# Spreading the filter taps over an iteration, and sums of squares on ScalarE

## What is computed

```python
q, k, v = silu(causal_dwconv(x @ W, w))            # 4 taps each
q = q * rsqrt(sum(q*q, -1) + 1e-6)                 # per head; k likewise
delta_out = delta_rule_chunkwise(q, k, v, beta)    # triangular solves, then a scan
fir_s = causal_dwconv(v, fir_short_w)              # 3 taps
fir_l = causal_dwconv(v, fir_long_w)               # 31 taps
hid = gelu(concat([x, fir_s, fir_l, delta_out]) @ W_fuse1 + b_fuse1)
logits = hid @ W_fuse2 + b_fuse2                   # softmax -> weights of four paths
o = p0*fir_s + p1*fir_l + p2*delta_out + p3*v
o = o * rsqrt(mean(o*o, -1) + 1e-5) * norm_w       # per head
out = o @ W_o
```

## Time and profile before

| | us |
|---|---|
| median of three runs | 2076.14 (2073.52 to 2077.61) |
| the profiled execution | 2078.35 |
| its span, first to last instruction | 2076.5 |

### The profile page before, as it was taken

How to read it: one execution, slowest core, us unless ns; L and a number is a source line. 1 busy time by engine, 2 the same in 40 slices (tenths; PEclk the granted TensorE clock), 3 DMA queues, 4 the chain that set the end, 5 groups by cost and what they waited for, 6 DMA issues and landing times. The chain is left out here.

```text
span 2076.5 us, 22850 instructions
## 1 busy us (share of the span) xinstructions
PE 1713.4 (83%) x8588; PEld 1154.6 (56%) x8588; DVE 997.7 (48%) x2206; ACT 542.2 (26%) x1180; POOL 758.3 (37%) x948
## 2 busy tenths in 40 slices
PE   4248888897878888888627999999995899999997
PEld 2226565655556565656423666666664455555554
DVE  3625878778687878777471111111101344444332
ACT  3123341514243342512122111111111222221221
POOL 1754556484655546472202333333322111111100
PEclk9667889797988888796867999999998999999999
DMA  3010111020111010020032333223312000000000
GB/s 100 16 21 16 21 37 31 2 59 8 46 21 47 21 46 11 6 51 32 0 132 81 81 82 80 60 43 75 78 18 43 1 21 21 21 21 21 1 11 21
DMA packets 108318, 77.99 MB, mean 38 GB/s; under 512 B 57384, under 2 KB 101424, under 8 KB 108208
## 3 DMA queue, kind: packets, MB, share of 16 engines
q1 hardware_dynamic: 95920, 59.74, 10.0%
q0 software_dynamic: 12288, 16.79, 4.7%
HBM read 51.34 MB, written 25.17 MB: 37 GB/s over the span
## 5 line engine op out<-in xcount | busy, mean ns | idle before, releaser
L383 DVE SCALAR_TENSOR_TENSOR a_firT<-a_v_ch,a_fir_lw,a_firT 128x511 f32<-128x511 f32 (+14 forms) x480 | 359.0, 817 | 0.0
L1505 DVE TENSOR_SCALAR ex_y<-ps,gT 128x256 f32<-128x256 f32 x64 | 31.0, 484 | 409.1 <-PE ps L1460 409.1
L1460 PE MATMUL ps<-ex_w,ex_hT 128*128 128x256 f32 x1024 | 223.5, 379 | 0.0
L1449 PE MATMUL ps<-ex_xT,ex_w 128*128 128x512 f32 x512 | 222.1, 594 | 0.0
L1460 PEld LDWEIGHTS ps<-ex_w,ex_hT 128*128 128x128 f32 x1024 | 194.0, 190 | 29.5 <-issue 3.8
L1415 POOL DMA_INDIRECT acc_dram<-ex_y,idxT x64 | 100.0, 1562 | 294.0 <-DVE ex_y L1505 294.0
L1487 ACT ACTIVATE ex_hT<-ps 128x512 f32<-128x512 f32 x128 | 76.4, 597 | 368.3 <-PE ps L1449 368.3
L1449 PEld LDWEIGHTS ps<-ex_xT,ex_w 128*128 128x128 f32 x512 | 97.7, 191 | 119.6 <-issue 119.2
L675 POOL TENSOR_TENSOR a_prod<-a_Yp,a_spare 128x126 f32<-128x126 f32 (+22 forms) x248 | 145.6, 587 | 29.7 <-DMA a_Yp<-y_dram 10.6
L1067 PE MATMUL ps<-a_firT,a_w_f 128*128 128x512 f32 x256 | 128.9, 628 | 18.3 <-DVE a_firT L383 18.3
L677 POOL TENSOR_TENSOR a_spare<-a_spare,a_prod 128x126 f32<-128x126 f32 (+22 forms) x248 | 116.3, 469 | 19.4
(11 more groups left out here) (275 smaller groups left out, 3061.7 us busy)
## 6 DMA issues: line engine op xcount, KB each, us to landing
ex_w<-in_L_ffn_w SPq DMA_DIRECT2D x16, 1024.0 KB, 8.9
a_xa<-in_L_attn_hidden_states SPq DMA_DIRECT2D x8, 512.0 KB, 4.3
a_xr<-in_L_attn_hidden_states SPq DMA_DIRECT2D x8, 512.0 KB, 4.7
a_Yp<-y_dram SPq DMA_DIRECT2D x16, 256.0 KB, 3.8
acc_dram<-a_xr SPq DMA_DIRECT2D x8, 512.0 KB, 4.5
xn_dram<-a_gxn SPq DMA_DIRECT2D x8, 512.0 KB, 3.2
l_xw<-acc_dram SPq DMA_DIRECT2D x8, 512.0 KB, 3.9
out<-l_xw SPq DMA_DIRECT2D x8, 512.0 KB, 2.9
```

The lines of the kernel that those rows point to most:

```text
L383: nc.vector.scalar_tensor_tensor(out[:, kind, c, s:], v, w[:, c, n - 1 - s:n - s], out[:, kind, c, s:], ALU.mult, ALU.add).then_inc(fir_st ...
L1449: ins = nc.tensor.matmul(ps[:, n % 4, :], w1[j][:, c, f * P:(f + 1) * P], xT[j][:, c, half * 512:(half + 1) * 512], start=c == 0, stop=c = ...
L1460: ins = nc.tensor.matmul(dn_slot(n), hT[half][:, f, (n % 4) * CAP:(n % 4 + 1) * CAP], w2[j][:, f, :], start=f == 0, stop=f == FB - 1)
```

## The change

`FIR_EARLY` goes from 40 to 20. Four of the 20 early taps stand ahead of scan(3), 16 behind it, and nothing is left behind the routing scores. The other 48 are spread over the next repetition: 3, 3, 5, 2, 10, 6 and 7 at seven places of `join` (`rest_of`), 2 ahead of scan(1), 5 ahead of scan(2) and 5 ahead of the end of the filters, where 18 stood in `join` and 10 in `main`. On VectorE the first two mixes come ahead of conv(b, 2), the last two and o_sums(e, 0) behind conv(b, 0) and ahead of their sums, and the second `masked_loc` comes behind `route_stats`. ScalarE squares each head's 64 columns with an instruction of its own that also sums them (`accum_out`): eight a tile in `kq_out`, four a tile in `out_squares`, 48 a repetition where eight stood. VectorE's eight reductions a repetition go. The semaphores that counted them are renumbered, and the squares wait for the powers of the image before.

```diff
--- before.py
+++ after.py
@@ -101,7 +101,7 @@
 PROJ = (2, 3, 0, 1, 4, 5)
 PROJ_BANK = (4, 5, 2, 3, 0, 1)
 NFIR = 2 * (TAPS_S + TAPS_L)
-FIR_EARLY = 40
+FIR_EARLY = 20
 NSOLVE = 3 + 2 * 31
 
 
@@ -437,11 +437,7 @@
 
             def kq_sums(b, p):
 
-                for t in (2 * p, 2 * p + 1):
-                    dve.wait_ge(sq_ready, b * 4 + t + 1)
-                    nc.vector.reduce_sum(ss[:, 8 * t:8 * t + 8], sq[t % 2][:].rearrange("p (h c) -> p h c", c=DK),
-                                         axis=AX.X).then_inc(ss_ready, 1)
-                dve.wait_ge(ss_ready, b * 6 + 3 * p + 2)
+                dve.wait_ge(sq_ready, b * 4 + 2 * p + 2)
                 nc.vector.tensor_scalar(ss[:, 16 * p:16 * p + 16], ss[:, 16 * p:16 * p + 16], 1e-6, None, ALU.add).then_inc(ss_ready, 1)
 
             def betas(b):
@@ -472,10 +468,7 @@
                                             spread(causal, 1, 2), ALU.mult).then_inc(loc_ready, 1)
 
             def o_sums(e, p):
-                for t in (2 * p, 2 * p + 1):
-                    dve.wait_ge(osq_ready, e * 4 + t + 1)
-                    nc.vector.reduce_sum(so[:, H * t:H * t + H], by_head(osq[:, t, :]), axis=AX.X).then_inc(so_ready, 1)
-                dve.wait_ge(so_ready, e * 6 + 3 * p + 2)
+                dve.wait_ge(osq_ready, e * 4 + 2 * p + 2)
                 nc.vector.tensor_scalar(so[:, 8 * p:8 * p + 8], so[:, 8 * p:8 * p + 8], 1.0 / DK, 1e-5, ALU.mult, ALU.add).then_inc(so_ready, 1)
 
             def o_norm(e, p):
@@ -538,68 +531,76 @@
                                         spread(rs[d % 2][:, t, H:2 * H], 2, DK), ALU.mult).then_inc(d_ready, 1)
 
             def join(b, d, e, r):
+                k = [FIR_EARLY]
+
+                def rest_of(n):
+                    if d is not None:
+                        fir(d, k[0], k[0] + n)
+                        k[0] += n
+
                 if e is not None:
                     rest = softmax_in(e)
                 if r is not None:
                     route_prob(r)
                 if e is not None:
                     rest()
-                if b is not None:
-                    conv(b, 2)
-                if e is not None:
                     mix(e, 0)
                     mix(e, 1)
+                if b is not None:
+                    conv(b, 2)
+                if e is not None:
                     mix_sum(e, 0)
                     mix_sum(e, 1)
                 if b is not None:
                     conv(b, 3)
+                rest_of(3)
+                if b is not None:
+                    conv(b, 0)
+                    betas(b)
                 if e is not None:
                     mix(e, 2)
                     mix(e, 3)
-                if b is not None:
-                    conv(b, 0)
-                    betas(b)
+                    o_sums(e, 0)
+                rest_of(3)
                 if e is not None:
                     mix_sum(e, 2)
                     mix_sum(e, 3)
-                    o_sums(e, 0)
-                if d is not None:
-                    fir(d, FIR_EARLY, FIR_EARLY + 6)
                 if b is not None:
                     conv(b, 5)
                 if e is not None:
                     o_norm(e, 0)
                     o_sums(e, 1)
+                rest_of(5)
                 if b is not None:
                     kq_sums(b, 0)
+                if e is not None:
+                    o_norm(e, 1)
+                rest_of(2)
+                if b is not None:
                     kq_sums(b, 1)
-                if e is not None:
-                    o_norm(e, 1)
-                if d is not None:
-                    fir(d, FIR_EARLY + 6, FIR_EARLY + 14)
+                rest_of(10)
                 if b is not None:
                     scales(b)
                     masked_loc(b, 0)
                 if e is not None:
                     add_out(e, 0)
-                if b is not None:
-                    masked_loc(b, 1)
+                rest_of(6)
                 if e is not None:
                     add_out(e, 1)
                     route_stats(e)
+                if b is not None:
+                    masked_loc(b, 1)
                 if b is not None and b + 1 < B:
                     norm_stats(b + 1)
-                if d is not None:
-                    fir(d, FIR_EARLY + 14, FIR_EARLY + 18)
+                rest_of(7)
 
             def main(b, d, e, nxt):
                 k = [0]
 
                 def more(n):
                     if b is not None:
-                        hi = min(FIR_EARLY, k[0] + n)
-                        fir(b, k[0], hi)
-                        k[0] = hi
+                        fir(b, k[0], k[0] + n)
+                        k[0] += n
 
                 if d is not None:
                     scan(d, 0)
@@ -608,15 +609,17 @@
                 if e is not None:
                     route_rows(e)
                 if d is not None:
+                    fir(d, FIR_EARLY + 36, FIR_EARLY + 38)
                     scan(d, 1)
-                    fir(d, FIR_EARLY + 18, FIR_EARLY + 23)
+                    fir(d, FIR_EARLY + 38, FIR_EARLY + 43)
                     scan(d, 2)
-                    fir(d, FIR_EARLY + 23, NFIR)
+                    fir(d, FIR_EARLY + 43, NFIR)
+                more(4)
+                if d is not None:
                     scan(d, 3)
-                more(18)
+                more(FIR_EARLY - 4)
                 if e is not None:
                     route_scores(e)
-                more(FIR_EARLY)
 
             norm_stats(0)
             norm_rows(0)
@@ -649,11 +652,11 @@
                 pool.tensor_tensor(rstd[:], var[:, 0, :], mhalf[:, 0:NT], ALU.pow).then_inc(rstd_ready, 1)
 
             def o_pow(e, p):
-                pool.wait_ge(so_ready, e * 6 + 3 * p + 3)
+                pool.wait_ge(so_ready, e * 2 + p + 1)
                 pool.tensor_tensor(ro[:, 8 * p:8 * p + 8], so[:, 8 * p:8 * p + 8], mhalf[:, 0:8], ALU.pow).then_inc(ro_ready, 1)
 
             def kq_pow(b, p):
-                pool.wait_ge(ss_ready, b * 6 + 3 * p + 3)
+                pool.wait_ge(ss_ready, b * 2 + p + 1)
                 pool.tensor_tensor(rs[b % 2][:, 2 * p:2 * p + 2, :], ss[:, 16 * p:16 * p + 16].rearrange("p (t h) -> p t h", t=2),
                                    mhalf[:, 0:16].rearrange("p (t h) -> p t h", t=2), ALU.pow).then_inc(rs_ready, 1)
 
@@ -741,9 +744,12 @@
             def kq_out(b, t):
 
                 act.wait_ge(kq_ps, b * 4 + t + 1)
-                if t >= 2:
-                    act.wait_ge(ss_ready, b * 6 + t - 1)
-                nc.scalar.activation(sq[t % 2][:], bank(2 + t), ACT.Square).then_inc(sq_ready, 1)
+                need(act, rs_ready, b * 2)
+                need(act, sq_ready, b * 4 + t - 1)
+                for h in range(8):
+                    ins = nc.scalar.activation(sq[t % 2][:, h * DK:(h + 1) * DK], bank(2 + t, h * DK, (h + 1) * DK), ACT.Square,
+                                               accum_out=ss[:, 8 * t + h:8 * t + h + 1])
+                ins.then_inc(sq_ready, 1)
                 nc.scalar.activation(k_tok[b % 2][:, t, :], bank(2 + t, 0, D), ACT.Copy).then_inc(k_ready, 1)
 
             def v_out(b, j, e):
@@ -796,7 +802,11 @@
             def out_squares(e, p):
                 for t in (2 * p, 2 * p + 1):
                     act.wait_ge(mix_ready, e * 8 + 2 * t + 2)
-                    nc.scalar.activation(osq[:, t, :], o[:, t, :], ACT.Square).then_inc(osq_ready, 1)
+                    need(act, ro_ready, e * 2)
+                    for h in range(H):
+                        ins = nc.scalar.activation(osq[:, t, h * DK:(h + 1) * DK], o[:, t, h * DK:(h + 1) * DK], ACT.Square,
+                                                   accum_out=so[:, H * t + h:H * t + h + 1])
+                    ins.then_inc(osq_ready, 1)
 
             def oT_out(e, t):
                 act.wait_ge(oT_ps, e * 4 + t + 1)
```

More of the change, by code:

```diff
@@ L546, in join @@
                     rest()
+                    mix(e, 0)
+                    mix(e, 1)
                 if b is not None:
@@ L549, in join @@
                 if e is not None:
-                    mix(e, 0)
-                    mix(e, 1)
                     mix_sum(e, 0)
@@ L555, in join @@
                     conv(b, 3)
-                if e is not None:
-                    mix(e, 2)
-                    mix(e, 3)
+                rest_of(3)
                 if b is not None:
@@ L562, in join @@
                 if e is not None:
+                    mix(e, 2)
+                    mix(e, 3)
+                    o_sums(e, 0)
+                rest_of(3)
+                if e is not None:
                     mix_sum(e, 2)
                     mix_sum(e, 3)
-                    o_sums(e, 0)
-                if d is not None:
-                    fir(d, FIR_EARLY, FIR_EARLY + 6)
                 if b is not None:
@@ L572, in join @@
                     o_sums(e, 1)
+                rest_of(5)
```

(7 more changed lines are left out.)

## The result

The changed kernel takes 2079.98 us (median of 9 runs, 2077.39 to 2084.24) against 2076.14 before: ratio 1.002, 95% interval 1.0012 to 1.0028, so slower by just the 0.2% that can be told. The forecast was 2056.0, faster, with a range of 2038 to 2088: the time is in the range and the sign is wrong. The profiled execution took 2084.24 (span 2082.4).

The account below looks back on a forecast made before the run. No engine is full; a chain changing engine sets the end, with TensorE waiting for inverses and logits. Six full repetitions -5, first -8, ninth -5.5, tenth -1: -19.5 us, median 2056, range 2038 to 2088.

Parts of the forecast that it names:

- stage B: TensorE's 32x32 products to the k/q transposes: faster products and projections, less squares and late mixes, -2.4 us a repetition.
- the last two repetitions: Ninth: shorter logits wait, less taps in its join, -5.5 us; tenth: sums wait one step less, -1 us.
- C: From the k/q transposes to the Gram products: head-by-head squares on ScalarE cost +5.3 us a repetition.
- D: From the Gram products to the scan's first mask: later second masking 1.2 and three more taps 2.0, +3.2 us.
- A: The stretch with TensorE's logits wait, up to the 32x32 products: the wait goes, -7.9 us a repetition.
- the wait that I blamed for it: TensorE's 7.93 us wait for the logits ahead of the 32x32 products, taken to lower its clock in the 8 us behind.
- The ten taps that I gave 0: VectorE's taps between kq_sums(1) and scales: no later than before, bounds -1 and +1.3 us, taken as 0.
- E: The rest of a repetition behind the scan's first mask: two taps ahead of scan(1), +0.9 us.
- The first repetition: GpSimd's first solve product, shut out by VectorE's stream of taps, ends sooner as the stream shortens: net -8 us.
- The rival that GpSimd is shut out in every repetition: Ten taps delay the power of kq_sums(1), seven times: +21, 2077; chance 0.12 shared with a slightly dearer pair.
- Taps can't be spread: Rival: VectorE is the bound, so nothing would move; no chance of its own given.
- a slightly dearer pair: ScalarE's square and accumulator read somewhat above 0.23 us: 2072 to 2080, the same; chance 0.12 shared with the shut-out.

Follow-up runs that it names:

- squares alone: The kernel before with only the accumulated squares, VectorE's sixteen reductions gone, taps and order as before: 2124.4 us.
- taps alone: The changed kernel with squares on ScalarE and reductions on VectorE as before, taps spread and steps in the new order: 2080.3 us.
- the pause: The kernel before, VectorE pausing behind its sixth early tap in the first repetition until GpSimd's first solve product and addition are done: 2066.8 us.
- the last kernel: The one with old squares, with four of five taps ahead of the scan moved into VectorE's idle time and the pause added: 1994.4 us.
- the one with old squares: The changed kernel with former squares and reductions, mixes ahead of taps, second masking ahead of last added output, 26 early taps: 2017.4 us.

## Why the prediction was wrong, step by step

Two steps failed: stage B, which was to be 2.4 us shorter a repetition and is 1.0 longer, and the last two repetitions. The sizes in C and D came out, but the terms behind them do not stand by themselves.

**A was right.** -7.8 for -7.9; TensorE's own work is next, as forecast.

**B failed, in two terms.** The first is "I take 1.3, as VectorE is ahead of TensorE by then": the wait for the mixes is 2.68, since the three taps take 3.71 beside GpSimd's convolution, a contention that the row used (0.65 a tap) does not have. The bounds, 0 and 4, held it. The second is "the two projection pairs 3.6 each instead of 5.47 and 5.36". The first of them came (3.70). The second did not, and could not: 5.36 stood in the earlier trace rows 14 us behind the wait that I blamed for it, with full clock in between (64 products in 2.11), and it is 5.40 with no wait. From rows: -1.3 for the products, -1.8 and +0.8 for the projections, +2.7 for the mixes and +0.7 more waiting for silu are +1.1, and +1.0 was measured.

**C was right in size and wrong in what it left out.** +4.4 for +5.3; the pair costs 0.24 and 0.19 for 0.23, and squares alone give +4.5. But "the eight reductions that leave VectorE buy nothing here, since ScalarE is last" was read from the old order. In the new one ScalarE would wait for them, as taps alone show. Summing the terms hid this: by them taps alone would be 7.4 us a repetition faster (-0.9 less 1.2 and 5.3), and they are 3.1 slower; squares beside them would be 6.5 slower, and are 0.9 faster. Two errors of 10.5 and 7.4 cancelled to 3.1.

**D was right in size and wrong in mechanism.** +3.5 for +3.2. I put 1.2 on the masking's place; moving it back makes the kernel slower, by 21 us in one place and some 5 in the other. TensorE waits there for the second masking, and VectorE then has statistics and seven taps left ahead of the scan's mask; the runs show no gain from taking away one of these alone. The ten taps that I gave 0 take 6.55 ahead of the scales. In the changed kernel ScalarE waits for the scales only twice (2.9 us in all); with taps alone it does eight times, for 12.4 us. The clock, which my D left out, moved as well: eight matmuls of TensorE's hidden layer there take 4.95 at a granted clock of 0.74, where they took 3.65 at 1.00 before.

**E** was +1.0 for +0.9.

**The first repetition: cause right, size off.** GpSimd is shut out by the stream there. In the changed kernel the first product again ends with the taps:

```profile
73.01 9.80 POOL L678 TENSOR_TENSOR a_prod<-a_Yp,a_spare 128x31 f32<-128x31 f32 x1 [3.03 <-DMA a_Yp<-y_dram]
...
76.04 6.66 DVE L383 SCALAR_TENSOR_TENSOR a_firT<-a_v_ch,a_fir_lw,a_firT 128x510 f32<-128x510 f32 x10
```

82.81 and 82.70, and the pause shows the cause. The second repetition's products start 9.5 us sooner (128.93 to 119.42), not 12 (13.1 less 1.0): I had left out that the first repetition pays for its own 32 pairs (its Gram products move from 51.5 to 55.4).

The rival that GpSimd is shut out in every repetition is out. The power of the second k/q sums starts 0.17 us into the ten taps that begin at 629.95 and ends three us before they do. In the eighth repetition the same product of the solve as above comes 3.7 us into seven taps, with GpSimd idle ahead of it, and is done half a us before they end:

```profile
630.12 3.32 POOL L660 TENSOR_TENSOR a_rs<-a_ss,const 128x16 f32<-128x16 f32 x1 [2.13 <-DVE a_ss L441]
...
887.48 4.55 DVE L383 SCALAR_TENSOR_TENSOR a_firT<-a_v_ch,a_fir_lw,a_firT 128x491 f32<-128x491 f32 x7
...
891.22 0.28 POOL L678 TENSOR_TENSOR a_prod<-a_Yp,a_spare 128x31 f32<-128x31 f32 x1 [2.94 <-DMA a_Yp<-y_dram]
```

So a stream does not always shut GpSimd out, and no run here shows what decides it.

**The last two repetitions failed.** Forecast -6.5; the ninth's products start 3.1 us sooner than before, its first scan mask is 2.9 later and attention ends 4.1 later. The failed step is "VectorE's idle takes over half" of the 18 taps: they stream ahead of the added outputs, and TensorE stands for those twice and then for the mask; the products of the earlier trace rows start at 938.00 without a wait, but then:

```profile
969.50 0.74 PE L1063 MATMUL ps<-const,a_dT 128*128 128x128 f32 x4 [2.88 <-DVE a_xr L485]
...
974.26 0.71 PE L1099 MATMUL ps<-a_uadj,a_k_tok 128*128 128x128 f32 x4 [1.45 <-DVE a_xr L485]
...
981.40 0.71 PE L1087 MATMUL ps<-a_S,a_nwT 128*128 128x128 f32 x4 [2.10 <-DVE a_S L528]
```

Putting the taps back shows that they earn 2.5 of the 5.5 at that mask and 0.7 at the end of attention; that the rest of the loss is the squares and taps of the eighth repetition (B to D +10.1 there, +6.1 by the forecast) rests on the traces alone.

**The account.** (By the prediction's own numbers the median is 2056.7, not 2056.) The forecast had -19.5 in all, and attention ends 4.1 later: 23.6 us are missing. Between the second and the seventh products it had 5 x -0.9 = -4.5, and +10.8 was measured (the periods in the trace add up to 592.0 for 581.2): 15.3 of the 23.6, with 5 x 3.4 from B and a little back from the rest; the other 8.3 lie in the first and the last repetitions. No rival named it. "Taps can't be spread" was wrong too, as the last kernel shows. The time lies where the forecast put a slightly dearer pair or GpSimd shut out by the ten taps, and that is chance: a pair takes 0.19 to 0.24, and GpSimd gets through.

## What to carry to other kernels

Costing the parts of a change one by one and adding them holds only while the engine that is last stays the same; where one part moves work ahead of what another part removes, cost the pair, in the new order. A slow row belongs to a wait only if nothing at full speed lies between them. Filler work goes into slots where its engine waits for another (there were 9.8 us of that in the changed kernel, and 1.5 and 1.9 in a repetition of the one with old squares), not ahead of anything that a second engine is about to need.

## What the runs showed of the hardware

In the first repetition GpSimd, arriving in the middle of an unbroken stream of VectorE instructions with two SBUF inputs, waited for the end of the stream (22.64 us through some thirty taps, 9.80 through some fifteen). In the eighth the same product got in ahead of the end, in 0.28, and in the sixth a power of 128x16 took 3.32 beside ten taps; what decides is not shown. GpSimd already running when the stream starts takes turns with it in the run with the pause, steps of 0.25 to 0.5 us becoming 0.57 to 0.8 and a tap 0.66 becoming 0.82. The Trainium skill's page "SBUF — State Buffer", section "Who interferes with whom", calls the ports that the two engines share an exclusive lock and has issue order decide who blocks; one instruction that comes second would then wait for one. The first repetition does not agree, since the block there was a whole stream; the taking of turns is in keeping with it.

TensorE's granted clock fell to a mean of 0.66 (partly 0.50, 1.2 GHz) in the eight projections behind 64 small products, with full clock (2.4 GHz) in the 5 us ahead and no wait between them; ahead of the small products TensorE had stood 0.99 us.

A square of 64 columns with an accumulator read follows the one before it by 0.19 us from PSUM and 0.24 from SBUF; eight of them take 1.6 from PSUM, where one square of 512 columns takes 0.48 to the next instruction, and 1.9 from SBUF, where two squares of 256 columns take 0.61.
